# Attention stage: rows of x transposed per block, tables spread over steps, residual DMAs issued by ScalarE

## What is computed

```
x = x + value_layer(layernorm(x))
x = x + ffn(layernorm(x))
x = x + attention(layernorm(x))      # 16 heads of 64, RoPE, windows of W = 128
x = x + ffn(layernorm(x))

q, k = rope(h @ Wq.T + bq), rope(h @ Wk.T + bk);  v = h @ Wv.T + bv
kcat, vcat = [previous block, own block]           # 256 keys for 128 queries
scores = q @ kcat.T / 8, band mask (kj >= qi) & (kj <= qi + W), block 0 sees its own block only
out = softmax(scores) @ vcat @ Wo.T + bo
```

## Time and profile before

| | |
|---|---|
| median of 3 runs | 1627.08 us (1626.82 to 1629.59) |
| the profiled execution | 1629.63 us, span of its instructions 1627.8 us |
| busy over the span | PE 92%, DVE 86%, ACT 81%, POOL 70% |
| mean granted TensorE clock | 0.979 |
| attention stage, PE's projections to its last product | about 204 to 1442 us |
| DMA issues of the stage on SP | `turn_p` x256, `turn_context` x64, `turn_x` x16, `load_x` x64, residual load x64, store x64, tables x32 |

### The profile page before, as it was taken

How to read it: one execution, slowest core, us unless ns; L and a number is a source line. 1 busy time by engine, 2 the same in 40 slices (tenths; PEclk the granted TensorE clock), 3 DMA queues, 4 the chain that set the end, 5 groups by cost and what they waited for, 6 DMA issues and landing times. The chain is left out here.

```text
span 1627.8 us, 46830 instructions
## 1 busy us (share of the span) xinstructions
PE 1503.2 (92%) x16866; PEld 1145.2 (70%) x16866; DVE 1403.6 (86%) x3859; ACT 1324.8 (81%) x2442; POOL 1137.7 (70%) x911
## 2 busy tenths in 40 slices
PE   5999878899999999999999999999999999869998
PEld 4888745576767676666767676767676767658887
DVE  5999668899989999999999898999898889857885
ACT  5999658888878888888888787888788878749996
POOL 4665367778777887878788777787787777623443
PEclk7999989999999999999999999999999999979999
DMA  5242247889998999999998999899989998962331
GB/s 210 92 124 99 65 100 128 169 164 176 169 183 159 176 161 184 165 187 170 170 184 157 172 166 169 168 176 172 173 151 175 165 166 159 172 157 69 109 111 70
DMA packets 728445, 247.92 MB, mean 152 GB/s; under 512 B 688148, under 2 KB 715032, under 8 KB 728216
## 3 DMA queue, kind: packets, MB, share of 16 engines
q1 hardware_dynamic: 727512, 244.53, 78.1%
q10 hardware_dynamic: 704, 0.40, 0.1%
HBM read 47.73 MB, written 25.17 MB: 45 GB/s over the span
## 5 line engine op out<-in xcount | busy, mean ns | idle before, releaser
L1283 DVE CUSTOM_DVE_ANT_0 at_prob<-banks,at_masks,pre_s_scale 128x256 f32<-128x256 f32 (+1 forms) x1024 | 421.3, 472 | 25.8 <-PE banks L1697 9.3
L1446 ACT ACTIVATE at_prob<-at_prob,at_top 128x256 f32<-128x256 f32 (+1 forms) x1024 | 428.3, 490 | 16.5 <-DVE at_top L1283 14.1
L1295 DVE TENSOR_TENSOR at_halves<-at_prob,at_halves 128x1024 f16<-128x1024 f32 (+1 forms) x256 | 331.7, 1296 | 3.1 <-ACT at_halves L1455 3.1
L1582 PE MATMUL banks<-at_xt,pre_w_h 128*128 128x512 f16 x1024 | 299.4, 385 | 12.4 <-ACT at_v_l L1474 7.6
L1697 PE MATMUL banks<-at_kt,at_qt 32*128 32x256 f32 (+1 forms) x4096 | 253.4, 384 | 31.5 <-issue 20.8
L1455 ACT ACTIVATE at_halves<-at_prob 128x1024 f16<-128x1024 f32 (+1 forms) x256 | 263.4, 1029 | 6.1
L1697 PEld LDWEIGHTS banks<-at_kt,at_qt 32*128 32x128 f32 x4096 | 198.6, 187 | 93.1 <-issue 88.4
L1653 PE MATMUL banks<-at_v_h,at_pt 128*128 128x65 f16 x1984 | 208.9, 195 | 32.7 <-DMA at_pt<-at_halves 25.8
L1653 PEld LDWEIGHTS banks<-at_v_h,at_pt 128*128 128x128 f16 x1984 | 182.1, 98 | 73.2 <-DMA at_pt<-at_halves 41.0
L1175 POOL TENSOR_TENSOR at_kt<-at_k_by 128x512 f32<-128x512 f32 x128 | 171.5, 1340 | 77.3 <-DVE at_halves L1295 65.6
L1165 POOL TENSOR_TENSOR at_q_by<-at_q_first,at_tables 128x512 f32<-128x512 f32 x128 | 175.5, 1375 | 61.5 <-DVE at_halves L1295 60.8
(11 more groups left out here) (123 smaller groups left out, 3319.1 us busy)
## 6 DMA issues: line engine op xcount, KB each, us to landing
f_x<-in_x SPq DMA_DIRECT2D x16, 512.0 KB, 3.7
x_after_ffn<-f_x SPq DMA_DIRECT2D x16, 512.0 KB, 2.7
at_x_res<-x_after_ffn SPq DMA_DIRECT2D x64, 128.0 KB, 3.1
x_after_attention<-at_x_res SPq DMA_DIRECT2D x64, 128.0 KB, 2.7
f_x<-x_after_attention SPq DMA_DIRECT2D x16, 512.0 KB, 4.4
out_x<-f_x SPq DMA_DIRECT2D x16, 512.0 KB, 3.0
at_x_ln<-x_after_ffn SPq DMA_DIRECT2D x32, 128.0 KB, 3.2
at_tables<-in_cos SPq DMA_DIRECT2D x16, 256.0 KB, 4.0
```

The costliest lines, as they stand in the source:

```text
L1283: last = nc.vector.tensor_tensor_reduce(out=prob[:, n % 2, h, low:2 * P], in0=s_ps[:, h, n % 2 * 2 * P + low:(n % 2 + 1) * 2 * P], in1=mas ...
L1295: nc.vector.tensor_tensor(parts[:, 1, :, :], prob[:, n % 2, :, keys_from(t, b):2 * P], parts[:, 0, :, :], ALU.subtract).then_inc(p_low, 1)
L1446: last = nc.scalar.activation(at, at, ACT.Exp, bias=top[:, n % 2, h:h + 1], scale=-1.0)
L1582: last = nc.tensor.matmul(pr_ps[:, half, :].rearrange("p (b t) -> p b t", b=SB), w[wp][:, k, at:at + P], xt[:, r, xp, :, k, :], start=n == ...
```

## The change

x is transposed per block: `x_halves` and `xt` get the block ahead of the half in their layout, and `turn_x(n)` transposes the 4 tiles of one block in each step (the first group still in one piece) where `turn_x(S)` did 16 tiles at `g == 0`. It is issued for n = t + 7, after `turn_p(t, 2)`. The two tables of a group are loaded in two steps, cos at `g == 3` and sin at `g == 1`, at the end of the step. `load_residual` and `store` are issued by ACT in its step, after `context_high`, up to step 63; SP does the rest of them. The rewording of `x_low_of`, `project` and `values` for the new layout is left out below.

```diff
-    x_halves = sb("x_halves", [P, 2, SB, C], F16)
-    xt = sb("xt", [P, 2, 2, SB, CK, P], F16)
+    x_halves = sb("x_halves", [P, SB, 2, C], F16)
+    xt = sb("xt", [P, 2, SB, 2, CK, P], F16)
...
+    def xt_turned(n):
+
+        S, blk = divmod(n, SB)
+        return 16 * (SB * (S // 2) + blk + 1) if S % 2 else 16 * (1 + SB * (S // 2 - 1) + blk + 1) if S else 16
+
     def xt_ready(S):
 
-        return 16 * (S // 2 + 1)
+        return xt_turned(SB * S + SB - 1)
...
-        def turn_x(S):
-
-            if big(S):
-                sp.wait_ge(x_low, SB * (S + 1))
+        def turn_x(n):
+
+            if step(n):
+                S, blk = divmod(n, SB)
+                sp.wait_ge(x_low, n + 1)
+                sp.wait_ge(xt_in[(n - 1) // SB % 2], xt_turned(n - 1))
                 need(v_done[1], NG * (S - 1))
-                if S < 2:
-                    sp.wait_ge(past.moved[S], past.stores(S + 2 * past.SLOTS))
-                sp.dma_start(xt[:, S % 2, :, :, :, :].rearrange("p e b k t -> p (e b k) t"),
-                             x_halves[:, :, :, :].rearrange("p e b c -> p (e b c)"),
+                if n == SB:
+                    sp.wait_ge(past.moved[1], past.stores(1 + 2 * past.SLOTS))
+                sp.dma_start(xt[:, S % 2, blk, :, :, :].rearrange("p e k t -> p (e k) t"),
+                             x_halves[:, blk, :, :].rearrange("p e c -> p (e c)"),
                              transpose=True).then_inc(xt_in[S % 2], 16)
...
         def at_step(t):
             S, g = divmod(t, NG)
             turn_p(t - 1, 3)
-            if g == 0:
-                turn_x(S + 1)
+            if t == -4:
+                first_turn_x()
             turn_context(t - 2)
             turn_p(t, 0)
-            load_residual(t - 4)
-            store(t - 6)
-            if g == 0 and S >= 0:
-                load_tables(S + 1)
             turn_p(t, 1)
             turn_p(t, 2)
+            if t + 7 >= SB:
+                turn_x(t + 7)
+            if t >= STEPS:
+                load_residual(t - 3)
+                store(t - 6)
             if t == -8:
                 load_x(SB)
             load_x(t + 13)
+            if g == 3 and S >= -1:
+                load_table(S + 2, 0)
+            if g == 1 and S >= 0:
+                load_table(S + 1, 1)
...
             context_high(t - 1)
+            store(t - 6)
+            load_residual(t - 3)
             if t + 8 >= SB:
                 normalize(t + 8)
                 x_high_of(t + 8)
```

More of the change, by code:

```diff
@@ L1071, in turn_context, with first_turn_x @@
                              transpose=True).then_inc(ct_in, 16)
[L1073 to L1076 removed]
+        def first_turn_x():
+            sp.wait_ge(x_low, SB)
+            sp.wait_ge(past.moved[0], past.stores(2 * past.SLOTS))
+            sp.dma_start(xt[:, 0, :, :, :, :].rearrange("p b e k t -> p (b e k) t"),
+                         x_halves[:, :, :, :].rearrange("p b e c -> p (b e c)"),
+                         transpose=True).then_inc(xt_in[0], 16)
+        def turn_x(n):
[3 more added lines that the diff above has]
+                sp.wait_ge(xt_in[(n - 1) // SB % 2], xt_turned(n - 1))
                 need(v_done[1], NG * (S - 1))
[L1078 to L1081 removed]
+                if n == SB:
+                    sp.wait_ge(past.moved[1], past.stores(1 + 2 * past.SLOTS))
+                sp.dma_start(xt[:, S % 2, blk, :, :, :].rearrange("p e k t -> p (e k) t"),
+                             x_halves[:, blk, :, :].rearrange("p e c -> p (e c)"),
                              transpose=True).then_inc(xt_in[S % 2], 16)
@@ L1101, in load_tables @@
                 at = SB * P * (S % SPB)
-                for e, table in enumerate((cos, sin)):
-                    sp.dma_start(tables[:, S % 2, e, :], table[:, at:at + SB * P]).then_inc(tab_in[S % 2], 16)
+                sp.dma_start(tables[:, S % 2, e, :], (cos, sin)[e][:, at:at + SB * P]).then_inc(tab_in[S % 2], 16)
         def load_residual(i):
@@ L1122, in opening @@
                 load_x(n)
-            load_tables(0)
+            load_table(0, 0)
+            load_table(0, 1)
             sp.dma_start(bv_cols[:, :], bv).then_inc(const_in, 16)
@@ L1528, in x_high_of, with load_residual, store @@
                 act.wait_ge(xn_made, n + 1)
-                need(xt_in[(S - 1) % 2], xt_ready(S - 1))
+                if S > 0:
+                    act.wait_ge(xt_in[(S - 1) % 2], xt_turned(n - SB))
                 if S == 0:
                     act.wait_ge(past.moved[5], past.stores(11))
-                nc.scalar.activation(x_halves[:, 0, blk, :], x_ln[S % 2][:, blk, :], ACT.Copy).then_inc(x_high, 1)
+                nc.scalar.activation(x_halves[:, blk, 0, :], x_ln[S % 2][:, blk, :], ACT.Copy).then_inc(x_high, 1)
+        def load_residual(i):
+            if step(i):
+                need(stored[i % RB], 16 * (i // RB))
+                if i < RB:
+                    act.wait_ge(past.low_made, 2 * past.CHUNKS)
+                act.dma_start(x_res[:, i % RB, :], x_in[:, i, :]).then_inc(res_in[i % RB], 16)
+        def store(i):
+            if step(i):
+                act.wait_ge(x_made, i + 1)
+                act.dma_start(x_out[:, i, :], x_res[:, i % RB, :]).then_inc(stored[i % RB], 16)
         def first_rows():
@@ L1599, in values @@
                             last = nc.tensor.matmul(
-                                pr_ps[:, half, blk * 2 * P:(blk + 1) * 2 * P], xt[:, r, xp, 2 * half + blk, k, :],
+                                pr_ps[:, half, blk * 2 * P:(blk + 1) * 2 * P], xt[:, r, 2 * half + blk, xp, k, :],
                                 w[wp][:, k, VC + g * 2 * P:VC + (g + 1) * 2 * P],
```

8 lines of the change are left out of this document (4 added, 4 removed).

## The result

| | before | after |
|---|---|---|
| median | 1627.32 us (1626.82 to 1629.59, 4 runs) | 1749.3 us (1747.61 to 1749.84, 4 runs) |
| ratio, 95% interval | | 1.0745, 1.0726 to 1.0764 |
| span of the profiled execution | 1627.8 us | 1748.0 us |
| mean granted TensorE clock | 0.979 | 0.946 |

A forecast was written before the change was run, and what follows sets the result against it. PE was taken to bound the undisturbed attention step at 18.42 us. Stalls lose 14 x 10.1 = 141 us and 41 come back, so 1627.1 + 100 = 1727 us, range 1699 to 1780.

The forecast's parts named there:

- The product waited for: On SP's queue, turn_x(t + 7) for a group's first block waits for values(t + 2, 1), computed in PE's step t + 1.
- The price of a stall: At PE's product of block 3: 8.1 us stall plus 2.0 behind it, 10.1 per group, 14 times, 141 us lost.
- The clock: After PE's standstill, 5.1 us at half speed lose 2.5 us; together with the late next block, 2.0 us.
- So the 41 us should come back: In the g == 0 steps, SP's crowding costs 15 x 2.7 = 41 us, nearly all won back; poor end 20.
- ACT's issues at 0: Residual load and store on ACT fit into its 2.19 us wait for PE's keys: 0 charged, up to 64 without cover.
- Rival (b): On ACT, issues take 2.39 us against 2.19 of cover, key_copy 0.2 late in 64 steps: 1740 us; no separate chance.
- (c): At PE's block 3, SP's lead covers the wait, so only the 41 us gain stays: 1586 us; chance 0.05.
- (d): At PE's stall, loss and gain cancel: about 3 us each if PE takes other work first; chance 0.03.
- Rival (a): The g == 0 excess is crowded DMA engines and only moves to other steps, 41 us stay lost: 1768 us; chance 0.09.

The follow-up runs named there:

- The first experiment's kernel: The kernel after with turn_x(t + 6) in place of turn_x(t + 7), nothing else; 1609.16 us against 1627.68 for the kernel before, ratio 0.9893.

## Why the prediction was right, and where it was off

**The product waited for: right.** SP stands at `turn_x` once in four steps until PE has ended `values(t + 2, 1)`, and behind it stand `load_x`, the sin table and `turn_p(t, 3)`. Changing 7 to 6 takes 134 us out of the `g == 2` steps.

**The price of a stall: right in the sum, by parts that cancel.** Forecast: a stall of 8.1 and 2.0 behind it, 141 us for 14. Measured: 134.4 us more in the `g == 2` steps and 6.3 in the `g == 3` ones, 140.7. That it agrees to the microsecond is luck: the stalls are 7.75 us on average, and the 0.45 per group lost in the step after was not forecast. Inside a step, the stall proper is 7.76 at 701.14. The quarter took 1.19 to issue where I took 1.0; the table 0.33 and `load_x` 0.52 instead of 0.42 and 0.80; the landing 5.1 instead of 5.5. SP was released within 0.1 us of PE's last `values` matmul, as assumed.

**The clock: right.** These are the stretches behind the stall, of the kernel after:

```profile
701.10:705.90 4.80, 4.76 (x41) 3.76 (x42) 1.74 (x3) 2.67 (x6) 0.00 (x0) 0.50 1.13 209
705.90:711.00 5.10, 5.10 (x75) 3.94 (x73) 3.10 (x8) 3.75 (x6) 0.00 (x0) 0.99 0.95 201
```

After the standstill PE runs at 0.50, the 1.2 GHz level, for 4.8 us, and then at the full one, as behind the stall in the kernel before. The step is 9.66 us over 18.42 (28.08), of which 7.76 are the stall and 1.9 what comes behind it: I had taken 2.0 for the clock and the next block together. But PE does not wait for the next block here. After the stall it waits over 0.3 us for a transpose in only 2 of the 14 steps (1.77 us in step 2, 0.38 in step 46), so nearly all of the 1.9 goes with the slow clock.

**"So the 41 us should come back": the term that was mis-sized.** 23 us came back, 20.0 in the `g == 0` steps and 3.2 in the `g == 1` ones. I had put the whole excess of those steps down to SP's crowded queue, with 20 us as the poor end. The trace of before already had a second cause beside it: POOL is busy 18.23 us of that step's 20.16, against 12.7 to 14.4 in its neighbours, and in the steps 16 and 32 of that kernel PE already waits 1.55 us for POOL's query and for no transpose. I read the row for the DMA share only. When the transposes of the probabilities come in time, PE waits for POOL's query next, in this timeline row of the kernel after:

```profile
662.85 0.71 PE L1733 MATMUL banks<-at_kt,at_qt 32*128 32x256 f32 x8 [1.55 <-POOL at_qt L1204]
```

Doubling the power on POOL added 12.5 us to these steps, so POOL's chain is on the path; taking the power out gave nothing back, so it is not alone there. By the traces DVE's long operation and ACT behind it then hold the step; why that operation is long, and so what sets those last 17 us, stays open. They were not reached by anything done to SP's queue here. And the parts do not add: of the 37 us in the `g == 0` steps, the transposes alone (without their stall) recover 18, the tables alone 15, the residual DMAs alone none, and all three 18 to 20. Why a given part helps is settled only in part: the transpose of x stood ahead of block 0 and the tables' data ahead of block 1, but that the gains overlap is measured, not derived. Nor was the queue all of it where it helped: what made block 1 late was the data of the tables on the DMA engines, and the 1.0 us of SP's issues moved to ACT gave nothing by itself.

**ACT's issues at 0: right.** The two issues over the whole kernel after (ns min/median/max), and ACT's timeline in its step 21:

```profile
L1566 ACTq DMA_DIRECT2D x_after_attention<-at_x_res x58: 325/326/345, 370.0 to 1548.3; - x58
...
L1560 ACTq DMA_DIRECT2D at_x_res<-x_after_ffn x61: 326/445/1299, 303.8 to 1548.7; - x61
```

```profile
678.69 0.58 ACT L1493 ACTIVATE at_v_l<-banks 128x512 f16<-128x512 f32 x1
678.98 0.33 ACTq L1566 DMA_DIRECT2D x_after_attention<-at_x_res  x1
679.17 0.58 ACT L1493 ACTIVATE at_v_l<-banks 128x512 f16<-128x512 f32 x1
679.34 0.44 ACTq L1560 DMA_DIRECT2D at_x_res<-x_after_ffn  x1
...
680.59 1.05 ACT L1513 ACTIVATE at_c_halves<-at_ctx 128x1024 f16<-128x1024 f32 x1
...
684.71 0.69 ACT L1522 ACTIVATE at_k_first<-banks,pre_bias 128x512 f32<-128x512 f32 x1 [2.13 <-PE banks L1618]
```

0.77 us for the pair, and the wait before the key copy is still 2.13 us (2.19 before). I had expected it to shrink to some 1 us. It did not because the issues take no time from the activations: both go out at 678.98 and 679.34, beside the low halves of the values and ahead of the context's high half (L1513, 680.59), which stands before them in the program. Rival (b) had 1740 for issues above 2.2 us; they are a third of that.

**The opening: not foreseen, 3.0 us.** In the opening, SP now has a quarter ahead of each of the last three loads of x, the first of them at 205.51. The last of the loads on the queue of the kernel after, and the same load in the kernel before:

```profile
211.93 0.51 SPq L1107 DMA_DIRECT2D at_x_ln_odd<-x_after_ffn  x1
```

```profile
205.78 0.42 SPq L1093 DMA_DIRECT2D at_x_ln_odd<-x_after_ffn  x1
```

That load leaves at 211.93 instead of 205.78. PE starts its step 0 3.0 us later. The first experiment's kernel has one quarter less there and starts it at 222.89, as before (222.66), so the early request goes with the delay. Its size is less sure: over all kernels that do not ask for the quarter at t + 7 this start lies between 221.8 and 224.7.

**The sum.** 140.7 - 23 + 3 = 120.7, against the forecast 141 - 41 = 100. (Three starts of steps are named one too high in the rows and the forecast: 546.17, 243.27 and 1360.83 begin the steps 17, 1 and 60. The stretch then has 15 steps of 17.9 and 44 of 18.42, and its excess is 38.6 us instead of 38.) The forecast of 1727 us is 22 below 1749.3, and 18 of these are the recovered term, 3 the opening. Rivals (c) and (d) are out, since the stall is there in full. Rival (a), 1768 with nothing back, is 19 us off where the forecast is 22, so its number was closer, by luck. It was wrong in that the excess would only move to other steps: 23 us came back, and the DMA engines moved 209 GB/s behind a stall, so 186 was no ceiling. It was right that part of the excess was in the transfers and not in SP's queue, as the tables showed.

## What to carry to other kernels

A wait on an in-order DMA queue is priced by what stands behind it and by when that is wanted: the same wait cost 135 us in front of one transpose and 36 us behind it. So before moving a request ahead, write down which count it asks for and in which step the other engine makes it; here one step of lead too many was the whole loss, and 7 changed to 6 turned 7.5% slower into 1.1% faster. And before booking an excess as recoverable, look for the second-latest engine in the same stretch, since that is where the gain stops.

## What the runs showed of the hardware

- Below 8 tiles of 128x128 the issue of a DMA transpose got no shorter: 4 tiles took as long as 8 tiles did before, 1.25 us, while the median over all transposes of probabilities, most of 16 tiles, was 2.1. All quarters of the kernel after, ns min/median/max, and their landing:

```profile
L1094 SPq DMA_TRANSPOSE at_xt<-at_x_halves x60: 1188/1210/1999, 205.5 to 1424.4; - x60
...
DMA to landing us min/median/max: 2.4/2.7/5.3
```

  Four quarters occupy SP for 4.8 us, one whole transpose for 2.64 in the crowded step.
- Plain DMAs of 128x256 were issued faster by ScalarE than by SP: 0.33 and 0.45 us against 0.43 and 0.58.
- ScalarE issued its two DMAs beside its own activations, at no cost to them: with both issues in them (678.98 and 679.34 above) the two low halves of the values took from 678.69 to 679.75, 1.06 us, against 1.05 before.
- When an elementwise operation of DVE and one of POOL overlapped, each mostly 1.2 to 1.4 us long, one of the two took 2.3. Moving POOL's work by a microsecond changed which one, in nine of ten steps.
